# Count matrices of a graph kernel: one pair product of 128 rows and 98 columns becomes two of 64 rows and 50 columns

## The reference, cut to what matters

```
edge_index = stack([src, dst]);  edge_index_t = stack([src, dst], axis=1)
h = maximum(layernorm(x), 0)
x = x + relu(segment_sum(w_norm * (h @ kernel)[dst], src) + bias)       # layer 0
h = maximum(layernorm(x), 0)
msg_fwd  = concat([h[src], edge_attr]) @ W_fwd  + b_fwd                 # layer 1
msg_back = concat([h[dst], edge_attr]) @ W_back + b_back
agg = segment_sum(concat([msg_fwd, msg_back]), concat([dst, src]))
out = x + layernorm(leaky_relu(agg / count) + h) * gamma + beta
```

## Time and profile before

| what | value |
|---|---|
| median of three runs | 6291.11 us |
| profiled execution | 6287.51 us, its span 6285.7 us |
| TensorE matmul busy over the span | 3579.1 us (57%) |
| VectorE / ScalarE / GpSimd busy | 3009.3 / 1906.9 / 2993.7 us |
| mean granted TensorE clock | 0.757 |
| `dense_sums`, from its first one-hot to its last add | 4815 to 6091 us |

### The profile page before, as it was taken

The page is one execution under the profiler, slowest core; times in us unless marked ns, Lnnn a source line. Parts: engine busy times, 40 slices in busy tenths (PEclk is TensorE's granted clock), DMA queues, the critical chain, the costliest instruction groups (busy, mean ns, idle before and its releaser), DMA issues. The chain is left out here.

```text
span 6285.7 us, 93695 instructions
## 1 busy us (share of the span) xinstructions
PE 3579.1 (57%) x27946; PEld 3167.1 (50%) x28096; DVE 3009.3 (48%) x4263; ACT 1906.9 (30%) x5027; POOL 2993.7 (48%) x1727
## 2 busy tenths in 40 slices
PE   0555000566666666666666666664012988888984
PEld 0444000565666556665566555664011766666764
DVE  3999000444444444444444444443134656565536
ACT  1011000333333333333333333332013545455532
POOL 0000000688888888888888888887301011110000
PEclk9777555777777777777777777776555999999997
DMA  3300029677777777777777777776333111110011
GB/s 74 24 18 18 18 98 273 141 137 137 133 134 137 137 135 134 136 137 137 135 133 137 137 137 134 134 137 109 100 103 110 35 35 35 35 35 25 5 36 54
DMA packets 687907, 622.18 MB, mean 99 GB/s; under 512 B 252021, under 2 KB 595789, under 8 KB 685852
## 3 DMA queue, kind: packets, MB, share of 16 engines
q0 software_dynamic: 234304, 213.56, 28.8%
q1 hardware_dynamic: 453432, 406.13, 22.2%
HBM read 327.05 MB, written 305.66 MB: 101 GB/s over the span
## 5 line engine op out<-in xcount | busy, mean ns | idle before, releaser
L497 POOL DMA_INDIRECT gcn_sums<-gw_sums,gw_to_i x1616 | 2750.8, 1702 | 1490.3 <-ACT gw_sums L643 1003.5
L581 PE MATMUL bank<-gw_window,gw_spread_hot 128*128 128x128 f32 x3232 | 793.4, 349 | 1291.4 <-DVE gw_spread_hot L539 1290.4
L581 PEld LDWEIGHTS bank<-gw_window,gw_spread_hot 128*128 128x128 f32 x3232 | 642.5, 255 | 1329.0 <-issue 809.3
L643 ACT COPY gw_sums<-bank 128x256 f32<-128x256 f32 x1616 | 601.9, 372 | 1465.6 <-PE bank L606 1169.8
L600 PE MATMUL bank<-gw_sum_hot,gw_attrs 128*128 128x128 f32 x3232 | 795.4, 336 | 395.5 <-DVE gw_sum_hot L543 198.0
L633 ACT ACTIVATE gw_pay<-bank,gw_rec 128x128 f32<-128x128 f32 x1616 | 593.5, 370 | 1160.2 <-PE bank L581 1139.6
L600 PEld LDWEIGHTS bank<-gw_sum_hot,gw_attrs 128*128 128x128 f32 x3232 | 629.1, 242 | 444.3 <-issue 444.3
L604 PE MATMUL bank<-gw_pay,gw_same 128*128 128x128 f32 x3232 | 757.1, 323 | 2.7 <-ACT gw_pay L633 2.6
L561 DVE CAST gw_to_i<-gw_to_f 128x8 int32<-128x8 f32 x202 | 34.9, 173 | 1481.2 <-DMA gcn_sums<-gw_sums,gw_to_i 1481.1
L606 PE MATMUL bank<-gw_attrs,gw_same 128*128 128x128 f32 x3232 | 744.0, 318 | 0.0
L604 PEld LDWEIGHTS bank<-gw_pay,gw_same 128*128 128x128 f32 x3232 | 625.8, 241 | 3.6 <-ACT gw_pay L633 2.9
(11 more groups left out here) (199 smaller groups left out, 4793.7 us busy)
## 6 DMA issues: line engine op xcount, KB each, us to landing
gw_attrs<-in_edge_attr SPq DMA_DIRECT2D x201, 512.0 KB
gw_rel_b<-dst_offset SPq DMA_DIRECT2D x202, 256.0 KB, 4.0
gw_key_b<-src_key SPq DMA_DIRECT2D x202, 256.0 KB
gcn_sums<-zeros SPq DMA_DIRECT2D x80, 640.0 KB
gcn_sums<-gw_sums,gw_to_i POOLq DMA_INDIRECT x1616, 3.8
n_part<-gcn_sums SPq DMA_DIRECT2D x16, 1562.5 KB
attr_by_dst<-gcn_sums SPq DMA_DIRECT2D x14, 1562.5 KB
gw_window<-g SPq DMA_DIRECT2D x202, 64.0 KB, 4.0
```

The lines of the kernel that those rows point to most:

```text
L497: nc.gpsimd.indirect_dma_start(out=tables[j % K], out_offset=bass.IndirectOffsetOnAxis(ap=to_i[:, h, j:j + 1], axis=0), in_=sums[:, h, j, ...
L581: nc.tensor.matmul(row_bank[j % 2][:, 0:F], spread_hot[:, h, j, :], window[:, h, :], start=True, stop=True).then_inc(row_ready, 1)
L643: nc.scalar.copy(sums[:, h, j, :], bank[j % B][:, 0:width]).then_inc(staged, 1)
```

## The change

The pair matmul of a place is split by tile. The low one-hot's upper 64 partitions and the high one-hot's upper 64 partitions are multiplied into one bank, the lower 64 into another (`HALF = 64`); since the two tiles no longer share a product, `hi` is used as it is and a one-hot of 50 columns is enough (`HH = NT`, 50; columns 0 to 48 are used). A batch is now eight places, 16 matmuls, over a pair of banks, and there are 16 batches per super tile. The pairs of banks take four of the eight PSUM banks, so `back_bank` is one bank where it was two, and the back product of each block waits for the add of the block before. The batches are spread by `ahead_of` (one or two per block, to block 11), and `FIRST_GO` and `AHEAD_GO` follow. ScalarE makes two copies of 392 elements per batch where it made one per batch of four places, so their number stays 800. In `gcn_nodes` two tensor_scalars on `hi` become one copy.

```diff
-HH = 2 * HI
+HH = NT
+HALF = P // 2
-                for b in range(2):
-                    last = nc.vector.tensor_scalar(hi[:, b:TILES:2, :], outside[:, b:TILES:2, :], 2.0, float(b), ALU.mult, ALU.add)
-                    last.then_inc(places_ready, 1)
+                nc.vector.tensor_copy(hi[:], outside[:]).then_inc(places_ready, 1)
...
-        PB = 4
+        PB = 8
-        pair_bank, row_bank, back_bank = d.bank[0:3], d.bank[3], d.bank[6:8]
+        pair_bank, row_bank, back_bank = (d.bank[0:2], d.bank[2:4]), d.bank[4], d.bank[7]
-        FIRST_GO = {1: 2, 2: 3, 4: 4, 5: 5, 6: 6, 8: 7}
-        AHEAD_GO = {10: 0, 11: 1}
+        FIRST_GO = {1: 2, 3: 3, 4: 4, 6: 5, 8: 6, 9: 7}
+        AHEAD_GO = {11: 0, 12: 1}
+        ahead_of = lambda b: [n for n in range(BATCHES) if n * (BLOCKS - 1) // BATCHES == b]
...
-                    last = nc.tensor.matmul(pair_bank[batch % B][:, c * HH:(c + 1) * HH], lo_hot[:, go % 2, q, :], hi_hot[:, go % 2, q, :],
-                                            start=True, stop=True)
+                    for b in range(2):
+                        node = slice(b * HALF, (b + 1) * HALF)
+                        last = nc.tensor.matmul(pair_bank[batch % B][b][:, c * HH:(c + 1) * HH], lo_hot[node, go % 2, q, :],
+                                                hi_hot[node, go % 2, q, :], start=True, stop=True)
...
-                    if not (first and h == 0 and b < 2):
-                        pe.wait_ge(src_added, u - 1)
+                    if not (first and h == 0 and b < 1):
+                        pe.wait_ge(src_added, u)
...
-                to = counts[:, h, :, :, :].rearrange("p t b q -> p (t b) q")[:, :, batch * PB:(batch + 1) * PB]
-                nc.scalar.copy(to, pair_bank[batch % B][:, 0:PB * HH].rearrange("p (c k) -> p k c", c=PB)).then_inc(pair_copied, 1)
+                for b in range(2):
+                    kept = pair_bank[batch % B][b][:, 0:PB * HH].rearrange("p (c k) -> p k c", c=PB)[:, 0:HI, :]
+                    last = nc.scalar.copy(counts[:, h, :, b, batch * PB:(batch + 1) * PB], kept)
+                last.then_inc(pair_copied, 1)
```

More of the change, by code:

```diff
@@ L873, in _ @@
             tiles(0)
-            pe.wait_ge(places_ready, 2)
+            pe.wait_ge(places_ready, 1)
             for n, (t0, t1) in enumerate(batches):
@@ L950, in dense_sums @@
         row_stage = sb("row_stage", [F, 2, 2 * P])
-        pair_bank, row_bank, back_bank = d.bank[0:3], d.bank[3], d.bank[6:8]
+        pair_bank, row_bank, back_bank = (d.bank[0:2], d.bank[2:4]), d.bank[4], d.bank[7]
         B = len(pair_bank)
-        turn_bank = [b[:].bitcast(BF16) for b in d.bank[4:6]]
+        turn_bank = [b[:].bitcast(BF16) for b in d.bank[5:7]]
         h1_in = [sem(f"h1_in{c}") for c in range(CHUNKS)]
@@ L1102, in add @@
                         dve.wait_ge(src_added, u - BLOCKS + 1)
-                    nc.vector.tensor_tensor(here, here, back_bank[(BLOCKS * h + b) % 2][:, 0:n], ALU.add).then_inc(src_added, 1)
+                    nc.vector.tensor_tensor(here, here, back_bank[:, 0:n], ALU.add).then_inc(src_added, 1)
             loop(dve, add, peeled=1)
@@ L1145, in products @@
                     turn(b + 1)
-                    ahead = [] if last else list(range(3 * b, min(3 * b + 3, BATCHES)))
+                    ahead = [] if last else ahead_of(b)
                     for k in range(wide(b)):
@@ L1169, in products @@
                         for s in range(3):
-                            ins = nc.tensor.matmul(back_bank[v][:, 0:n], now[:, h, half, s, :], turned[:, v, half, 0:n],
+                            ins = nc.tensor.matmul(back_bank[:, 0:n], now[:, h, half, s, :], turned[:, v, half, 0:n],
                                                    start=(half == 0 and s == 0), stop=(half == 1 and s == 2))
@@ L1204, in copies @@
                     if not last:
-                        for batch in range(3 * b, min(3 * b + 3, BATCHES)):
+                        for batch in ahead_of(b):
                             keep_counts(t + 1, 1 - h, batch, first=(first and h == 0))
```

## The result

The changed kernel takes 6313.26 us as the median of seven runs (6307.86 to 6315.57) against 6290.06 of before: a ratio of 1.0035, 95% interval 1.0024 to 1.0047, +23 us. Its profiled span is 6313.8 us, 28.1 more than before; that execution was the longest of its seven. The sign was forecast; the forecast size was +55 us.

What follows compares the result with a forecast made beforehand. The prediction took TensorE to bound the kernel. Shapes +84, pair matmuls -37, the single back bank +18 and VectorE -10 made +55 us on the profiled 6287.5, so 6342.5, about 6345 as median; range 6236 to 6415 us.

Steps and rivals of the forecast that it cites:

- The sign: Whole kernel: slower than before, given 0.68, against 0.24 for faster and 0.08 for same.
- What bounds: In `dense_sums`, TensorE bounds: what is added to or taken from its stream moves the end; VectorE's savings stay mostly hidden.
- The pair matmuls: TensorE's bound stream, 3072 places: 0.033 us per place instead of 0.045, -37 us, between -58 and +22.
- Changes of shape: Entering and leaving each pair-matmul group on TensorE: 0.11 us per change, 768 changes, +84 us, bounds 0 to +123.
- One back bank: Block 12's back product waits for block 11's add, behind a go: 0.75 us, 24 times, +18 us, bounds +7 to +24.
- Behind it wait the transposes of the next super tile: At a super tile's end, block 12's late back product delays the next transposes; counted in +18 us, nothing for the jump.
- VectorE: High one-hots 0.4 us shorter: stalls -6 us, super tile 0 about -4; -10 in the sum, -15 to +30 kept.
- Rival B: Pair matmuls: changes of shape cost 0.11 us and halves run in a line, +114 us, 6405 us; chance 0.22.
- A: Pair matmuls: changes of shape cost nothing and halves run side by side, -50 us, 6241 us; chance 0.27.
- C: Pair matmuls: changes of shape cost nothing and halves run in a line, +30 us, 6321 us; chance 0.13.

Runs made afterwards that it cites:

- after_wide_hot: The changed kernel with the high one-hot still made 98 columns wide, the matmuls using 50 of them: 6324.1 us, ratio 1.0063 to before.
- after_halves: The changed kernel with every batch of 16 pair matmuls issued as two groups of eight, a row product between: 6378.9 us, ratio 1.0129 to before.
- after_groups: The changed kernel with a go's two batches issued together, 32 pair matmuls per group, goes a block earlier at most: 6289.5 us, ratio 0.9997 to before.
- before_one_bank: The kernel before with one back bank instead of two, nothing else of the change: 6334.8 us, ratio 1.0061 to before.
- after_spare: The changed kernel with block 12's back product in the idle first pair bank and two goes moved a block earlier: 6285.1 us, ratio 0.9988 to before.
- after_no_adds: The changed kernel without GpSimd's 14 adds of tables, their loads kept: 6271.7 us, ratio 0.9968 to before.
- after_full_rows: The changed kernel with both pair matmuls of a place taking all 128 rows, so the shape never changes: 6319.0 us, ratio 1.0037 to before.

## Why the prediction was right or wrong

- *What bounds* held: every change of the stream's starts showed in the end, while of the 124 us less of high one-hots on VectorE after_wide_hot finds some 17 at the end.
- *The pair matmuls*: -37 us forecast between -58 and +22, measured 24 x 16 x 0.143 = -55. The halves run side by side; I had taken 0.033 us per place, and it is about 0.028 in a group of eight places (0.0255 for each further one).
- *Changes of shape*: +84 forecast from two half-clock rows, measured 384 x 0.195 = +75 from the starts and 0.209 per group in after_halves. The mechanism and size held, at full clock and with bf16 too.
- *One back bank*: +18 forecast, +19 measured in its direct part, 0.79 us each. The reason was partly wrong: the add at 5782.83 is not behind a one-hot, VectorE had been idle for 0.30 us. The wait is the back product's latency and the add itself, and moving a go does not remove it (after_groups). That the size came out is in part luck.
- *Missing*, the first step that failed: "Behind it wait the transposes of the next super tile" was as far as I followed it, so the jump stood at nothing in the sum. The wait stands ahead of the loop's jump, which lost its cover: +27 us, about half of it idle time, while the rest fits the lower clock behind it; it is shown by before_one_bank and by the profile of after_spare.
- *VectorE*, the second step that failed: the sum's -10, with "I keep -15 to +30 us" for the stalls. Measured -40 from the stalls and their clock and -3 at the start. I priced a shorter one-hot and left out the clock behind a stall. The traces show that TensorE wants the held go later, and after_no_adds shows what that is worth; what made it later is open.

75 - 55 + 19 + 27 - 43 = +23. Two errors of some 30 us with opposite signs, +27 and -33, nearly cancel by luck, and what is left of the miss, 55 against 23, is the pair matmuls (-18), the shapes (-9), the bank (+1) and the rest of these two (-6). Rival B (halves in a line) and A and C (shapes free) are refuted by after_full_rows and after_halves.

## What to carry to other kernels

The 64-row matmuls did run side by side, but entering and leaving them cost about 0.1 us each way: make the groups long enough, here 16 matmuls just fail to pay and 32 pay. A semaphore wait right ahead of the loop's end cost more than its own length, because the jump, 3.4 us here, is free only as far as work is queued ahead of it. And a kernel with stalls that come at a fixed time gives back part of what is added ahead of them: compare the stretches with and without the disturbance before a total is explained.

## What the runs showed that I had not expected

- TensorE's sequencer needs 3.3 to 4.1 us for a jump back over 1930 to 2420 instructions, and some 24 instructions behind it TensorE is idle for another 1.4 to 3.6 us (4.0 to 5.8 behind the seventh jump), in every kernel with the loop.
- Removing this jump is worth 50 us to the kernel before and 108 us to the changed one, and turns the verdict on the change from 23 us slower to 34 us faster, through the stalls at GpSimd's adds.
- With the loop written out, the clock fell to 1.2 GHz with 13 of 13 stalls of 4.5 us idle time, and with three of 15 stalls of 1.0 to 2.2 us.
